# A selective scan's softplus: the logarithm on ScalarE, with the rounding of 1 + e put back, in place of a polynomial of degree 9 on VectorE

## The reference, cut to what matters

```python
def _mamba_forward(x, in_proj_w, conv_w, conv_b, x_proj_w, dt_proj_w, dt_proj_b, out_proj_w, A_log, D_param):
    combined = x @ in_proj_w
    u, x_gate = jnp.split(combined, 2, axis=-1)
    ...
    u = jax.nn.silu((u_c + conv_b[None, :, None]).transpose(0, 2, 1))
    x_dbl = u @ x_proj_w
    delta, b, c = jnp.split(x_dbl, [D_INNER, D_INNER + D_STATE], axis=-1)
    delta = jax.nn.softplus(delta @ dt_proj_w + dt_proj_b)
    a = -jnp.exp(A_log)
    def step(h, inp):
        u_t, d_t, b_t, c_t = inp
        h = jnp.exp(d_t[:, :, None] * a) * h + d_t[:, :, None] * b_t[:, None, :] * u_t[:, :, None]
        y_t = jnp.einsum('bds,bs->bd', h, c_t)
        return (h, y_t)
```

## Time and profile before

| | us |
|---|---|
| median of three runs | 2980.59 (2976.67 to 2988.99) |
| the profiled execution, its own time | 2991.93 |
| its span | 2990.1 |
| TensorE busy in the span | 2753.9 (92%) |
| VectorE busy | 1495.6 (50%) |
| ScalarE busy | 985.3 (33%) |
| softplus stage, its first matmul to the next stage's barrier | 2446.9 to 2541.1 |
| scan stage, to the end of its scans | 2541.1 to about 2788 |

### The profile page before, as it was taken

How to read it: one execution, slowest core, us unless ns; L and a number is a source line. 1 busy time by engine, 2 the same in 40 slices (tenths; PEclk the granted TensorE clock), 3 DMA queues, 4 the chain that set the end, 5 groups by cost and what they waited for, 6 DMA issues and landing times. The chain is left out here.

```text
span 2990.1 us, 46350 instructions
## 1 busy us (share of the span) xinstructions
PE 2753.9 (92%) x18066; PEld 1931.0 (65%) x18066; DVE 1495.6 (50%) x2520; ACT 985.3 (33%) x2204; POOL 151.0 (5%) x302
## 2 busy tenths in 40 slices
PE   8888978999998989699999979789999987999899
PEld 4666964666666579456666769646767743767445
DVE  4573234777777430345454462444445437899500
ACT  2332224666664213322222212222222223666100
POOL 1002021010010010100000010200000000000000
PEclk9989988999999989899999989999999998999999
DMA  9235852111111039321111037321111000222000
GB/s 299 87 110 182 299 194 66 44 30 44 30 30 46 1 120 325 106 75 46 64 64 44 31 115 262 104 88 64 43 64 64 33 37 1 78 71 71 32 1 14
DMA packets 96792, 259.99 MB, mean 87 GB/s; under 512 B 18916, under 2 KB 44232, under 8 KB 89048
## 3 DMA queue, kind: packets, MB, share of 16 engines
q1 hardware_dynamic: 85512, 240.17, 24.1%
q0 software_dynamic: 3840, 10.49, 1.1%
q10 hardware_dynamic: 7248, 6.65, 0.7%
HBM read 236.13 MB, written 21.14 MB: 86 GB/s over the span
## 5 line engine op out<-in xcount | busy, mean ns | idle before, releaser
L2183 DVE TENSOR_REDUCE buf<-acc 128x1 f32<-128x1024 f32 x128 | 150.7, 1219 | 367.1 <-PE acc L2077 367.1
L2152 ACT ACTIVATE buf<-acc,buf 128x1024 f32<-128x1024 f32 x128 | 142.7, 1115 | 365.4 <-DVE buf L2183 365.4
L2071 PE MATMUL acc<-buf 128*128 128x512 f32 x512 | 239.9, 612 | 21.7 <-DMA buf<-in_ctxT 18.3
L356 PE MATMUL acc<-buf 128*128 128x256 f32 (+4 forms) x768 | 229.9, 494 | 14.7 <-PEq L86 14.7
L2097 PE MATMUL acc<-buf 128*128 128x256 f32 x1024 | 231.7, 379 | 1.5 <-ACT buf L2162 1.5
L2097 PEld LDWEIGHTS acc<-buf 128*128 128x128 f32 x1024 | 190.7, 190 | 25.7 <-issue 1.9
L356 PEld LDWEIGHTS acc<-buf 128*128 128x128 f32 (+2 forms) x768 | 134.4, 193 | 112.1 <-issue 103.6
L2199 DVE COPY buf<-acc 128x1024 f32<-128x1024 f32 x128 | 156.1, 1220 | 91.9 <-PE acc L2086 91.9
L2562 DVE TENSOR_REDUCE buf<-acc 128x1 f32<-128x512 f32 x256 | 159.0, 683 | 77.4 <-PE acc L2440 77.4
L2528 ACT ACTIVATE buf<-acc,buf 128x512 f32<-128x512 f32 x256 | 172.6, 686 | 75.0 <-DVE buf L2562 75.0
L2071 PEld LDWEIGHTS acc<-buf 128*128 128x128 f32 x512 | 94.0, 194 | 127.2 <-issue 102.2
(11 more groups left out here) (388 smaller groups left out, 4440.8 us busy)
## 6 DMA issues: line engine op xcount, KB each, us to landing
buf<-in_L_ffn_W SPq DMA_DIRECT2D x52, 1024.0 KB, 6.6
buf<-in_ctx SPq DMA_DIRECT2D x48, 768.0 KB, 4.4
buf<-in_ctxT SPq DMA_DIRECT2D x64, 512.0 KB, 5.5
buf<-in_L_ffn_w SPq DMA_DIRECT2D x36, 704.0 KB, 5.8
buf<-state_rows SPq DMA_DIRECT2D x32, 512.0 KB, 3.6
buf<-in_ctxT SPq DMA_DIRECT2D x96, 128.0 KB, 5.5
buf<-in_L_ffn_w SPq DMA_DIRECT2D x18, 640.0 KB, 6.5
buf<-in_ctxT SPq DMA_DIRECT2D x32, 256.0 KB, 5.2
```

What stands on the lines that cost most here:

```text
L356: ins = pe.matmul(banks[n % nbanks][rows(r), 0:w], lhsT, rhs, start=(k == 0), stop=(k == len(pairs) - 1))
L2071: pe.matmul(acc_s[y][:, halves(h)], q0[:, b, 2 * r:2 * r + 2, :], ct0[x][:, halves(h)], start=True, stop=False)
L2152: act.activation(probs[u % 4][:, :], acc_s[u % 2][:, :], ACT.Exp, bias=negmax[:, u % 4:u % 4 + 1], accum_out=total[:, u % 4:u % 4 + 1]).th ...
L2183: dve.tensor_reduce(negmax[:, u % 4:u % 4 + 1], acc_s[u % 2][:, :], AX.X, ALU.max, negate=True).then_inc(max_ready, 1)
```

## The change

The polynomial and its coefficients go. VectorE now makes 1 + e (`pm`, rounded), and from it the rounding error (pm - 1) - e, which it subtracts from max(z, 0); ScalarE takes the logarithm of `pm` into the buffer `du`; VectorE adds it and multiplies by u. The work of a half is now in two passes: `raise_by_one` of both quarters, then `finish` of both. ScalarE takes the two logarithms of a half right behind its exponents, and TensorE's turn(1) and its copy move ahead of step(1) and exponents(1). The wait of the idle products falls away.

```diff
@@ TensorE
                     turn(0)
+                    turn(1)
                     step(1)
-                    turn(1)
                     turn(2)
-                    pe.wait_ge(links, 4 * (len(coef) + 1) - 5)
                     idle_products(chip, pe, acc_z[0], 4)
                     turn(3)
@@ ScalarE
+                    def logarithm(q):
+                        h, r = q // 2, q % 2
+                        to, pm = (t[:, 2 * r:2 * r + 2, halves(h)] for t in (du, p))
+                        act.wait_ge(raised, q + 1)
+                        act.activation(to, pm, ACT.Ln).then_inc(log_done, 1)
...
                     keep_low(0)
                     exponents(0)
+                    logarithm(0)
+                    logarithm(1)
                     keep_low(1)
                     act.wait_ge(rows_turned, 1)
                     act.copy(brows[:, :, :], acc_rows[:, :, 0:NS])
                     keep_turned(0)
+                    keep_turned(1)
                     exponents(1)
-                    for q in range(1, 4):
+                    logarithm(2)
+                    logarithm(3)
+                    for q in range(2, 4):
                         keep_turned(q)
@@ VectorE
-                    for q in range(4):
...
-                        dve.wait_ge(exp_done, h * C + 2 * r + 2)
-                        chain.link(dve.tensor_scalar(pm, em, coef[-1], None, ALU.mult))
-                        for k in coef[-2::-1]:
-                            chain.link(dve.scalar_tensor_tensor(out=pm, in0=pm, scalar=k, in1=em, op0=ALU.add, op1=ALU.mult))
-                        chain.link(dve.scalar_tensor_tensor(out=z, in0=z, scalar=0.0, in1=pm, op0=ALU.max, op1=ALU.add))
+                    def raise_by_one(q):
+                        em, pm, z, _, _ = part(q)
+                        dve.wait_ge(exp_done, q // 2 * C + q % 2 * 2 + 2)
+                        chain.link(dve.tensor_scalar(pm, em, 1.0, None, ALU.add))
+                        dve.sem_inc(raised, 1)
+                        chain.link(dve.scalar_tensor_tensor(out=em, in0=pm, scalar=-1.0, in1=em, op0=ALU.add,
+                                                            op1=ALU.subtract))
+                        chain.link(dve.scalar_tensor_tensor(out=z, in0=z, scalar=0.0, in1=em, op0=ALU.max, op1=ALU.subtract))
+
+                    def finish(q):
+                        em, pm, z, up, dup = part(q)
+                        dve.wait_ge(log_done, q + 1)
+                        chain.link(dve.tensor_tensor(z, z, dup, ALU.add))
                         dve.tensor_tensor(dup, z, up, ALU.mult).then_inc(du_ready, 1)
+
+                    for h in range(2):
+                        for q in (2 * h, 2 * h + 1):
+                            raise_by_one(q)
+                        for q in (2 * h, 2 * h + 1):
+                            finish(q)
```

More of the change, by code:

```diff
@@ L2622, in _ @@
                 statistics.close(dve)
[L2625 to L2631, removed]
 def selective_scan_front(chip, w):
@@ L2701, in selective_scan @@
             e, p, du = (ib(P, C, T) for _ in range(3))
-            coef = log1p_coefficients()
             with Stage(chip) as st:
@@ L2708, in selective_scan @@
                 acc_rows = st.psum(P, NT, 2 * NS)
-                (projected, low_ready, filled, magnitude, exp_done, links, du_ready, turned, copied, rows_turned,
-                 kept) = st.sems(11)
+                (projected, low_ready, filled, magnitude, exp_done, links, raised, log_done, du_ready, turned, copied,
+                 rows_turned, kept) = st.sems(13)
                 block = st.block()
@@ L2810, in _, with part @@
                     chain = Chain(dve, links)
-                    for q in range(4):
+                    def part(q):
                         h, r = q // 2, q % 2
-                        em, pm, z, up, dup = (t[:, 2 * r:2 * r + 2, halves(h)] for t in (e, p, delta, u, du))
-                        dve.wait_ge(exp_done, h * C + 2 * r + 2)
-                        chain.link(dve.tensor_scalar(pm, em, coef[-1], None, ALU.mult))
-                        for k in coef[-2::-1]:
-                            chain.link(dve.scalar_tensor_tensor(out=pm, in0=pm, scalar=k, in1=em, op0=ALU.add, op1=ALU.mult))
-                        chain.link(dve.scalar_tensor_tensor(out=z, in0=z, scalar=0.0, in1=pm, op0=ALU.max, op1=ALU.add))
-                        dve.tensor_tensor(dup, z, up, ALU.mult).then_inc(du_ready, 1)
+                        return (t[:, 2 * r:2 * r + 2, halves(h)] for t in (e, p, delta, u, du))
+                    def raise_by_one(q):
[10 more added lines that the diff above has]
+                        chain.link(dve.tensor_tensor(z, z, dup, ALU.add))
+                        dve.tensor_tensor(dup, z, up, ALU.mult).then_inc(du_ready, 1)
+                    for h in range(2):
[3 more added lines that the diff above has]
+                            finish(q)
         early.close()
```

## The result

Twenty runs of each: 2973.64 us for the changed kernel (2968.25 to 2984.28), 2982.49 us for the kernel before (2976.67 to 2988.99). The ratio is 0.9976, with a 95% interval from 0.9967 to 0.9985, so 7 us less (4 to 10); the two medians themselves lie 8.9 us apart. That is within 0.5%, where the prediction had put it, and inside its range of 2962 to 2979 us. The 10.3 us of its sum lie just outside the interval.

What follows compares the result with a forecast made beforehand. VectorE's last two quarters were taken to bound the softplus stage's tail. Last product 11.8 us earlier, less 2.45 for idle products, plus 0.9 for turn(3) at full clock: 10.3 us saved, 2980.6 to 2970.3 us, range 2962 to 2979.

Steps and rivals of the forecast that it cites:

- The tail is VectorE's, the first half is hidden: Softplus stage: VectorE's last two quarters set the time, its first two run beside TensorE; the whole gain is quarter 3.
- Turn(1) ahead of step(1) costs 2.2 us: TensorE, softplus stage: turn(1) waits for the copy of turn(0), so step(1) and exponents(1) come 2.2 us later.
- The four table loads cost nothing at 1.28 each: ScalarE, softplus and scan stages: each of four table loads takes 1.28 us and is absorbed by slack.
- The rival that a switch costs about double: ScalarE: each table switch costs 1.28 us more than its row; saving 9.9 us, so 2970.7; chance 0.08.
- The last product, 43.2 us behind T0 by the forecast: VectorE, end of softplus stage: quarter 3's product ends at 2525.95, 8.2 us behind the last Exp; before, 2537.76.
- The idle products in the way of turn(3): TensorE, end of softplus stage: idle products run right behind turn(2) and delay turn(3) by 2.45 us.
- The scan stage unchanged: Scan stage: the fourth load costs nothing and drive(0) runs at half clock as before; first scan released by TensorE.
- The rival with the clock up into the scan stage: TensorE, scan stage: drive(0) takes 2 us, not 4, and 1.5 us more are saved: 11.8, so 2968.8; chance 0.12.
- The logarithm's table from afar: ScalarE: the logarithm's table loads are fetched from memory; at 10 us a load 2997, slower than before; chance 0.04.

Runs made afterwards that it cites:

- log_first_half: Kernel before with only the first half's two quarters by logarithm, the second by polynomial, turn(1) behind step(1); last copy at 58.08 us, ratio 0.9998.
- log_second_half: Kernel before with only the second half's two quarters by logarithm, the first by polynomial, turn(1) behind step(1); last copy at 45.83 us, ratio 0.9949.
- poly3: Kernel before with a polynomial of degree 3 in place of 9, so a less exact softplus; last copy at 42.98 us, ratio 0.9958.
- turn1_back: Changed kernel with turn(1) back behind step(1) and its copy behind the logarithms; last copy at 46.41 us, ratio 0.9937.
- no_rounding: Changed kernel without the two instructions per quarter that put the rounding of 1 + e back, so less exact; last copy at 46.35 us, ratio 0.9963.
- extra_loads: Changed kernel with a one-element square root ahead of logarithm(0) and logarithm(2), forcing two further table loads; last copy at 49.38 us, ratio 0.9969.
- scan_warm: Changed kernel with four idle products as TensorE's first instructions in the scan stage; third scan 10.98 us behind the last copy, ratio 0.9974.
- no_idle: Changed kernel without the four idle products between turn(2) and turn(3); last copy at 47.27 us, ratio 0.9952.
- by_quarter: Changed kernel with the second half done quarter by quarter and turn(1) behind step(1), two more table loads; last copy at 41.38 us, ratio 0.9935.
- kept_warm: Changed kernel with sixteen idle products ahead of turn(2) replacing the four behind it, and four at the scan stage's start; last copy at 46.52 us, ratio 0.9944.
- by_quarter_warm: by_quarter with idle products added: six behind turn(1), eight behind turn(2), four at the scan stage's start; last copy at 41.33 us, ratio 0.9946.

## Why the prediction was right

*The tail is VectorE's, the first half is hidden.* Shown: log_first_half (nothing), log_second_half (all of it), poly3 (12 instructions, 15.1 us).

*Turn(1) ahead of step(1) costs 2.2 us.* Shown by turn1_back, 2.17. Step(1) began 19.25 us behind T0, by the forecast at 2501.9 - 2482.73 = 19.2.

*The four table loads cost nothing at 1.28 each.* Right for the second and third by the timelines of after. The slack of the third was 0.9 by the forecast; no_rounding shows 1.1 (two instructions, 2.5 us, less in quarter 3 brought 1.07 before the wait for a logarithm came out), extra_loads 1.0 (1.50 more cost 0.50). Right for the first too: its slack was 1.2 by the forecast and is 1.1 by extra_loads (1.50 more cost 0.39). The fourth hid behind drives at half clock, and scan_warm shows it as the next bound. The rival that a switch costs about double has fallen: load and activation stand back to back in every trace. The Trainium skill, "ScalarE: Activation LUTs", section "What ACT_TABLE_LOAD costs", with its drain of 1380 ns, doesn't agree with extra_loads, where no more than 0.02 us stands ahead of a load or behind it; the trace decides. The Trainium skill, "ScalarE: Activation LUTs", section "Table sets: the hidden batching unit", has Exp and the logarithm in one set, at one load; here a load of 1.28 us stands between them each time.

*The last product, 43.2 us behind T0 by the forecast*, came at 43.47. The missing 0.25 are three small steps: the last Exp ended 0.04 later than forecast, VectorE began 0.11 us behind it where the forecast had left nothing, and 0.85 us and not 0.72 lie between the start of 1 + e and the next instruction, where raising `raised` stands.

*The idle products in the way of turn(3)* were rightly put on the path and mis-sized. The term had 2.45 us for them, by a clock that rises after some 4 us of work, and turn(3) at 1.04. It rose 5.6 us after turn(2) began; turn(3) started 46.3 behind T0 and not 45.7, and took 1.23. That is the step that failed in size: 9.5 us saved to the last copy and not 10.3.

*The scan stage unchanged*: nearly. The third scan came 0.5 us later, with the second waiting 0.39 us for drive(1). The cause is the moment at which the clock rose behind the start of drive(0): 4.0 us before, 5.5 in the changed kernel, where it was up at 2526.8:

```profile
2526.00:2528.00 2.00, 2.00 (x15) 1.97 (x15) 1.61 (x2) 1.47 (x5) 0.00 (x0) 0.79 0.00 0
```

The third scan follows this moment in kernels that all have the fourth load: with 3.4 us it is 12.32 behind the last copy (no_idle), with 5.0 it is 12.69 (log_second_half), with 6.1 it is 13.24 (by_quarter). So the load is not what cost these 0.5 us. It makes 9.0 in all. The rival with the clock up into the scan stage didn't occur: it fell before drive(0).

*The logarithm's table from afar*: didn't occur, its loads take 1283 ns.

By the traces the change saves 9.0 us of 2982, a ratio of 0.9970, inside both timed intervals; forecast were 10.3. The 1.3 us between them are the 0.8 of the idle products and turn(3) and the 0.5 of the scan stage, both mainly from when the clock rises. The median came out at 2973.6 and not at 2970.3: these 1.3 us, and 1.9 because the median of three runs that the forecast starts from was low (2980.6 against 2982.5 of twenty). The range of 17 us would have held much smaller and larger savings, so that the time fell into it says little; it is the trace that bears the mechanism out.

## What to carry to other kernels

In a stage that ends on one engine's tail, count only what that engine has to do behind its last input: a cheaper method is worth its saving there and nothing in the part that another engine covers. The same logarithm, ordered by quarter and with turn(1) where it was, saved 15.9 us by the trace (ratio 0.9935) against 9.0, though it loads two tables more. Of these 6.9 us, 2.1 are turn(1) (turn1_back) and 4.8 the order by quarter; look at order before arithmetic. When a wait falls away, look at what it held back: filler that used to run inside a wait now ran ahead of work that was ready, and turn(1), which had been free in a gap, was paid for.

## What was not expected of the hardware

The moment at which TensorE's clock changes can't be had from one trace. It rose 3.8 us after work began in the earlier trace rows and 5.6 in the changed kernel, 3.2 in no_rounding. It fell 2.5 to 3.4 us into gaps of the earlier trace rows, yet in kept_warm behind a gap of 1.3 us, with 7 us of idle products shortly before. Behind drive(1) TensorE waits 1.97 us in scan_warm and in by_quarter_warm alike: the clock fell there in the second and not in the first. Windows of kept_warm around turn(3), and as the next stage begins (columns as in the earlier trace rows):

```profile
2534.00:2536.00 2.00, 1.09 (x8) 0.86 (x8) 1.97 (x3) 0.20 (x1) 0.00 (x0) 1.00 0.00 0
2536.00:2538.00 2.00, 0.94 (x5) 0.94 (x6) 1.01 (x1) 0.81 (x1) 0.00 (x0) 0.77 0.00 0
2540.00:2542.00 2.00, 1.56 (x4) 1.32 (x5) 0.10 (x2) 1.67 (x7) 0.00 (x0) 0.50 0.04 18
```

What decides it stays open. It is worth 1 to 2 us each time, as much as many an edit.
